# Products that nobody reads in three idle times of TensorE, in a two-layer kernel of attention and experts

## The chip, the cores and the metric

The kernel runs on one core of one Trainium2 chip. Its time is device microseconds of one launch, the median of three runs: 1240.93 us (1238.18 to 1246.87). Lower is better.

## The reference, cut to what matters

Two layers over 4 x 1024 tokens of 128 channels, each block followed by a layer norm with the residual:

```python
x = _layernorm(x + _L0_attn_ref(...))  # linear attention, elu + 1, 16 heads of 8
x = _layernorm(x + _L0_ffn_ref(...))   # 8 experts, 128 -> 512 -> 128, silu, top 2, capacity ceil(1.2 N / E)
x = _layernorm(x + _L1_attn_ref(...))  # causal softmax attention with alibi, 16 heads of 8
x = _layernorm(x + _L1_ffn_ref(...))   # 32 experts, top 4, and a shared expert
```

The third line decides most of the time: for each of 4 batches and 16 heads, 1024 x 1024 scores (the lower triangle), the largest of each query's row, exp of the difference, the product with v, and the projection. The experts of the second line each take at most a fixed number of tokens, gathered by index.

## The kernel before, in words

The program is a row of stages, each a block in which every engine has its own list of instructions; a stage ends when all engines have ended it. The stages are linear attention, routing, the first experts (`stage_experts0`), the second attention (`stage_attention`) and the second experts.

**First experts.** GpSimd (POOL) gathers 5 tiles of 128 rows for each of 8 experts, at most 2 gathers in flight. For each expert TensorE turns the 5 tiles (line 920), computes the hidden layer in four parts c = 0 to 3 of 640 columns each (512 and 128, line 935, float32), turns the tiles of the next expert, and computes the output (line 947, 20 products). ScalarE copies the turned rows (line 956) and takes silu of each part (line 968); part c = 2 waits for the silu of part 0, because two pairs of PSUM banks take turns. The order on TensorE is the order in which the code stands.

**Second attention, its start.** GpSimd gathers batch 0's expert outputs (line 1457), VectorE combines them pair by pair (line 1469, with the sums of the norm behind it), POOL takes the root (line 1443), ScalarE scales the rows (line 1406), TensorE turns them (line 1340) and makes q, k and v (lines 1343 and 1346, the list `QKV_UNITS`). ScalarE copies q and k out (lines 1395 and 1399) and splits each into three bf16 parts together with VectorE (lines 1418, 1424, 1430). SP and ScalarE issue transfers that put the parts of batch 0 into the operands `qa` and `ka` (line 1103).

**First maxima.** Attention goes in 16 steps of 4 heads. Before a step's exps, the maxima of its rows must be known: a list `MAX_UNITS` of 40 units of score products (lines 2017 for the mask and 2019), each reduced by VectorE (line 2209), and one last unit that turns the maxima (line 2006) so that they can be sent by DMA as rows of `qa` (line 1860). The units use the three PSUM banks 4, 5 and 7 in turn, so a unit's products wait until the unit three before it is reduced. For step 0 all 41 units stand ahead of the steps, and 8 units of step 1 (`EARLY`) behind them, which need the operands of step 1; these come through DRAM (`q_steps`, `k_steps`). VectorE works on other sums between these units. Inside the steps, the units of the following step stand between the score products (lines 2035 and 2039), the exps of ScalarE (line 2147) and the products with v (line 2054). Each engine has its order written out by hand; semaphores join them.

The matrix `G.ident` is a 128 x 128 identity in float32.

Of the kernel before, what the change touches and what calls it, by code (L numbers as in the profile page):

```python
# [24 lines left out]
P = 128  # L25
# [3 lines left out]
TB = SEQ // P  # L29
# [5 lines left out]
E0, H0, K0 = 8, 512, 2  # L35
# [86 lines left out]
def wait_landed(engine, landed, count):  # L122

    ahead = len(landed)
    for u in range(ahead):
        if count > u:
            engine.wait_ge(landed[u], (count + ahead - 1 - u) // ahead * 16)
# [712 lines left out]

class Weights0:


# [18 lines left out]
def stage_experts0(nc, G, I, S, W):  # L864
    HC = H0 // P
    ST = SLOTS0 // P
    FIRST = min(SLOTS0, HALF)
    PARTS = ((0, FIRST), (FIRST, SLOTS0))
    RING = 3
    with ExitStack() as ctx:  # L870
        M = Mem(nc, ctx)
        two, ring = range(2), range(RING)
        w1, w2, b1, b2, w_here = W.w1, W.w2, W.b1, W.b2, W.here
        rows = [M.sb(f"rows_{v}", [P, ST, C]) for v in ring]
        xT = [M.sb(f"exT_{u}", [P, SLOTS0]) for u in two]
        hT = M.sb("hT", [P, HC, SLOTS0])
        y = [M.sb(f"ey_{u}", [P, ST, C]) for u in two]
        landed, y_kept = [M.sem(f"landed{u}") for u in range(AHEAD)], [M.sem(f"y_kept{u}") for u in two]
        xT_psum, xT_done, h_psum, h_done = M.sem("xT_psum"), M.sem("xT_done"), M.sem("h_psum"), M.sem("h_done")
        y_psum, y_done = M.sem("y_psum"), M.sem("y_done")  # L880
        B = G.bank
        with nc.Block() as block:
            @block.gpsimd
            def _(pool):
                spaced = Spaced(pool, landed)
                for e in range(E0):
                    if e >= RING:
                        pool.wait_ge(xT_psum, e - RING + 1)
                    for s in range(ST):
                        spaced.start(out=rows[e % RING][:, s, :], out_offset=None, in_=G.x_dram,  # L890
                                     in_offset=bass.IndirectOffsetOnAxis(ap=G.token0[:, e * ST + s:e * ST + s + 1], axis=0),
                                     bounds_check=N - 1)

            @block.sync
            def _(sp):
                def keep(e):
                    sp.dma_start(G.expert_out0[e * SLOTS0:(e + 1) * SLOTS0, :].rearrange("(s p) c -> p s c", p=P),
                                 y[e % 2][:]).then_inc(y_kept[e % 2], 16)

                for e in range(2, E0):  # L900
                    sp.wait_ge(y_psum, e - 1)
                    W.load_in(sp, I, e)
                    sp.wait_ge(y_done, e - 1)
                    W.load_bias(sp, I, e)
                    keep(e - 2)
                for e in range(E0 - 2, E0):
                    sp.wait_ge(y_done, e + 1)
                    keep(e)
                for u in two:
                    sp.wait_ge(y_kept[u], E0 // 2 * 16)  # L910

            @block.tensor
            def _(pe):
                def turn(e):
                    wait_landed(pe, landed, (e + 1) * ST)
                    if e:
                        pe.wait_ge(xT_done, e)
                    for s in range(ST):
                        c, at = divmod(s * P, HALF)
                        mm = pe.transpose(B[c][:, at:at + P], rows[e % RING][:, s, :], G.ident[:])  # L920
                    mm.then_inc(xT_psum, 1)

                turn(0)
                for e in range(E0):
                    u = e % 2
                    pe.wait_ge(xT_done, e + 1)
                    pe.wait_ge(w_here[u], (e // 2 + 1) * 64)
                    for c in range(HC):
                        if c < 2:
                            if e:  # L930
                                pe.wait_ge(h_done, e * HC)
                        else:
                            pe.wait_ge(h_done, e * HC + c - 1)
                        for n, (a, b) in enumerate(PARTS):
                            mm = pe.matmul(B[2 + 2 * (c % 2) + n][:, 0:b - a], w1[u][:, c * P:(c + 1) * P],
                                           xT[u][:, a:b], start=True, stop=True)
                        mm.then_inc(h_psum, 1)
                    if e + 1 < E0:
                        turn(e + 1)
                    if e:  # L940
                        pe.wait_ge(y_done, e)
                    for s in range(ST):
                        n, at = divmod(s * C, HALF)
                        for c in range(HC):
                            if s == 0:
                                pe.wait_ge(h_done, e * HC + c + 1)
                            mm = pe.matmul(B[6 + n][:, at:at + C], hT[:, c, s * P:(s + 1) * P], w2[u][:, c, :],  # L947
                                           start=(c == 0 and at == 0), stop=(c == HC - 1), skip_group_check=True)
                    mm.then_inc(y_psum, 1)

            @block.scalar
            def _(act):
                def copy(e):
                    act.wait_ge(xT_psum, e + 1)
                    for n, (a, b) in enumerate(PARTS):
                        last = act.activation(xT[e % 2][:, a:b], B[n][:, 0:b - a], ACT.Copy)
                    last.then_inc(xT_done, 1)

                copy(0)
                for e in range(E0):  # L960
                    u = e % 2
                    act.wait_ge(w_here[u], (e // 2 + 1) * 64)
                    if e:
                        act.wait_ge(y_psum, e)
                    for c in range(HC):
                        act.wait_ge(h_psum, e * HC + c + 1)
                        for n, (a, b) in enumerate(PARTS):
                            last = act.activation(hT[:, c, a:b], B[2 + 2 * (c % 2) + n][:, 0:b - a], ACT.Silu,
                                                  bias=b1[u][:, c:c + 1])
                        last.then_inc(h_done, 1)  # L970
                    if e + 1 < E0:
                        copy(e + 1)

            @block.vector
            def _(dve):
                for e in range(E0):
                    u = e % 2
                    dve.wait_ge(y_psum, e + 1)
                    dve.wait_ge(w_here[u], (e // 2 + 1) * 64)
                    if e >= 2:  # L980
                        dve.wait_ge(y_kept[u], e // 2 * 16)
                    for n, (a, b) in enumerate(PARTS):
                        k = (b - a) // P
                        last = dve.tensor_tensor(y[u][:, a // P:b // P, :], B[6 + n][:, 0:b - a].rearrange("p (s c) -> p s c", c=C),  # L984
                                                 b2[u][:, None, :].to_broadcast([P, k, C]), ALU.add)
                    last.then_inc(y_done, 1)
# [44 lines left out]
MAX_UNITS = max_units()  # L1031
SLOTS = len(EXP_UNITS)
EARLY = 8
# [93 lines left out]
def step_plan():  # L1127

    def flags(n):
        return n == 0, n + 1 < STEPS, n + 2 < STEPS  # L1130
    count = lambda n: sum(map(len, schedule(*flags(n))))
    base = [len(MAX_UNITS) + EARLY]
    for n in range(STEPS):
        base.append(base[-1] + count(n))
    return flags, base
# [90 lines left out]
    return b == BATCH - 1 and c == 1 and kind in ("turn_att", "proj", "turn_new")  # L1226


SECOND_MOMENTS_AT = 26


# [599 lines left out]
def stage_attention(nc, G, I, S):  # L1831
# [3 lines left out]
    with ExitStack() as ctx:  # L1835
        M = Mem(nc, ctx)
        Q = Qkv(M, G.w_gu)
# [12 lines left out]
        PS, B = G.psum, G.bank  # L1850
        Q.small_read = small_read
        OUT = 6
        _, base_of = step_plan()
# [9 lines left out]
        with nc.Block() as block:  # L1863
# [121 lines left out]
            @block.tensor  # L1985
            def _(pe):
                pe.wait_ge(S.weights, 11 * 16)
                for kind, c in QKV_UNITS:
                    emit_side_tensor(pe, S, Q, (kind, 0, c))
                pe.wait_ge(G.mask_rows_here, 2 * SIDES * 16)  # L1990
# [69 lines left out]
                number = 0  # L2060
                for s, units in ((Step(0, 0, 0), MAX_UNITS), (Step(1, 1, 0), MAX_UNITS[:EARLY])):
                    for u in units:
                        emit_small(number, number % 2, s, ("max", 0, u))
                        number += 1

                def body(s, base, odd, flags):
                    pe.wait_ge(max_here[s.buf], s.used * 48 + 48)
# [89 lines left out]
            def _(dve):  # L2157
# [67 lines left out]
                for s, units in ((Step(0, 0, 0), MAX_UNITS), (Step(1, 1, 0), MAX_UNITS[:EARLY])):  # L2225
                    for u in units:
                        if number == SECOND_MOMENTS_AT:
                            dve.wait_ge(Q.summed, 4)
# [721 lines left out]
```

## Time and profile before

| | us |
|---|---|
| median of the runs | 1240.93 |
| lowest and highest run | 1238.18, 1246.87 |
| the profiled execution's own time | 1239.79 |
| its span, from first to last instruction | 1238.0 |
| TensorE busy in the span | 956.7 (77%) |
| VectorE busy | 795.7 (64%) |
| ScalarE busy | 545.5 (44%) |
| mean granted clock of TensorE | 0.878 of 2.4 GHz |

Busy time is that of instructions on an engine, matmuls with their way through the array. The granted clock is 1.00 at 2.4 GHz and 0.50 at 1.2 GHz; a value between them is a stretch with both. A line of the timeline gives the start, the time from the first start to the last end of the merged instructions, the engine, the line of the kernel, what is written from what, the shape, the count, and in brackets how long the engine had been idle and what ended that.

### The profile page before, as it was taken

What the parts mean: (1) busy time and instruction counts of PE and PEld (TensorE: products, weight loads), DVE (VectorE), ACT (ScalarE), POOL (GpSimd) and SP (SyncE); (2) the same over time, 40 slices, a digit from 0 to 9 for tenths busy, and PEclk for the clock granted to TensorE, in tenths of its full rate; (3) what the DMA queues carried; (4) which work ended last, traced back from release to release, by engine and by line L of the source; (5) the groups of instructions that cost most, each with busy time, mean ns of one, the idle gap of its engine ahead of it and who ended that gap; (6) DMA issues with size and microseconds to landing.
All of it is one profiled execution on the core that took longest, in us unless ns stands there. A gap on an engine that the chain in (4) does not pass through costs nothing. (4 is left out here: it accounts for less than half of the span.)

```text
span 1238.0 us, 20993 instructions
## 1 busy us (share of the span) xinstructions
PE 956.7 (77%) x7024; PEld 549.2 (44%) x7024; DVE 795.7 (64%) x2147; ACT 545.5 (44%) x878; POOL 488.6 (39%) x484
## 2 busy tenths in 40 slices
PE   5772118980489899998999898888889989998971
PEld 3662016760223333343334343332278868874541
DVE  4767770014397789788988888979356524554653
ACT  1331003431207667766667574555653434431241
POOL 3101045515622710262006430243545545556776
PEclk9985558995659999999989898998899999998996
DMA  4224102421311200120012222053166746541132
GB/s 119 69 69 161 30 7 79 130 71 34 88 59 35 96 29 31 43 96 28 34 41 70 79 81 80 21 156 122 53 189 190 216 138 176 170 112 43 46 83 57
DMA packets 113439, 106.19 MB, mean 86 GB/s; under 512 B 17770, under 2 KB 95210, under 8 KB 112696
## 3 DMA queue, kind: packets, MB, share of 16 engines
q1 hardware_dynamic: 74216, 65.53, 17.5%
q0 software_dynamic: 12048, 25.71, 7.7%
q10 hardware_dynamic: 27072, 13.64, 3.8%
q8 instruction: 57, 0.93, 0.3%
q14 instruction: 46, 0.38, 0.1%
HBM read 59.60 MB, written 41.94 MB: 82 GB/s over the span
## 5 line engine op out<-in xcount | busy, mean ns | idle before, releaser
L2209 DVE TENSOR_REDUCE maxima<-psum 128x1 f32<-128x512 f32 (+3 forms) x640 | 375.5, 626 | 58.8 <-PE psum L2019 57.6
L2147 ACT ACTIVATE probs<-psum 128x1024 f32<-128x1024 f32 (+3 forms) x384 | 294.5, 810 | 190.8 <-PE psum L2039 188.7
L2019 PE MATMUL psum<-ka,qa 61*128 61x512 bf16 (+3 forms) x768 | 219.7, 353 | 8.3 <-DVE maxima L2209 6.8
L2039 PE MATMUL psum<-qa,ka 64*128 64x512 bf16 (+3 forms) x768 | 169.9, 342 | 4.3 <-ACT probs L2147 3.7
L2054 PE MATMUL psum<-probs,v_wide 128*32 128x512 f32 (+3 forms) x1536 | 170.5, 518 | 0.7 <-ACT outT L2118 0.6
L1531 POOL DMA_INDIRECT sorted<-x_rows,to_row x76 | 75.9, 999 | 195.4 <-DVE to_row L1686 101.8
L2017 PE MATMUL psum<-mask 64*128 64x128 bf16 x512 | 100.1, 232 | 32.3 <-DMA qa<-max_parts 10.3
L2564 ACT ACTIVATE g_silu<-psum 128x512 f32<-128x512 f32 x80 | 47.8, 597 | 175.4 <-PE psum L2470 101.7
L1457 POOL DMA_INDIRECT w_gu<-expert_out,to_row x64 | 65.1, 1017 | 124.7 <-ACT probs L2147 84.8
L2019 PEld LDWEIGHTS psum<-ka,qa 61*128 61x128 bf16 x768 | 68.0, 98 | 96.0 <-DVE maxima L2209 73.4
L2470 PE MATMUL psum<-w_gu,g_xT 128*128 x384 | 96.8, 395 | 9.1 <-DVE g_h L2640 5.4
L2017 PEld LDWEIGHTS psum<-mask 64*128 64x128 bf16 x512 | 44.9, 97 | 132.6 <-DVE maxima L2209 88.5
L118 POOL DMA_INDIRECT f_got<-expert_out,dense x64 | 64.5, 1008 | 66.2 <-DMA f_got<-expert_out,dense 46.7
L2035 PE MATMUL psum<-mask 64*128 64x128 bf16 x512 | 85.5, 229 | 3.2 <-ACT probs L2147 2.3
L2640 DVE TENSOR_TENSOR g_h<-psum,g_silu 128x512 f32<-128x512 f32 x48 | 33.2, 691 | 77.6 <-ACT g_silu L2564 77.4
L2470 PEld LDWEIGHTS psum<-w_gu,g_xT 128*128 128x128 f32 x384 | 70.1, 192 | 25.4 <-issue 17.6
L2775 POOL DMA_INDIRECT f_got<-expert_out,dense x64 | 65.1, 1017 | 21.6 <-issue 21.6
L118 POOL DMA_INDIRECT sorted<-x_rows,to_row x52 | 51.2, 985 | 55.9 <-DMA sorted<-x_rows,to_row 38.4
L2039 PEld LDWEIGHTS psum<-qa,ka 64*128 64x128 bf16 x768 | 56.6, 98 | 29.4 <-ACT probs L2147 13.4
L984 DVE TENSOR_TENSOR ey<-psum,b 128x512 f32<-128x512 f32 (+1 forms) x16 | 7.1, 486 | 88.1 <-PE psum L947 88.1
L118 POOL DMA_INDIRECT rows<-x_dram,token x40 | 40.0, 1000 | 44.9 <-DMA rows<-x_dram,token 27.5
L2054 PEld LDWEIGHTS psum<-probs,v_wide 128*32 128x32 f32 x1536 | 31.0, 110 | 49.7 <-issue 42.1
(326 smaller groups left out, 1619.4 us busy)
## 6 DMA issues: line engine op xcount, KB each, us to landing
g_rows<-sorted SPq DMA_DIRECT2D x192, 64.0 KB
expert_out<-g_y ACTq DMA_DIRECT2D x48, 256.0 KB
w<-in_W SPq DMA_DIRECT2D x16, 256.0 KB, 3.1
w_gu<-in_gu SPq DMA_DIRECT2D x4, 1024.0 KB, 10.8
sorted<-blank SPq DMA_DIRECT2D x54, 64.0 KB
q_steps<-w_gu SPq DMA_DIRECT2D x12, 256.0 KB
k_steps<-w_gu SPq DMA_DIRECT2D x12, 256.0 KB
qa<-q_steps SPq DMA_DIRECT2D x30, 96.0 KB
```

Of the source, the lines that this page charges most:

```text
L118: self.pool.indirect_dma_start(oob_is_err=False, **transfer).then_inc(self.landed[u], 16)
L1457: pool.indirect_dma_start(out=Q.got[:, t, k, :], out_offset=None, in_=G.expert_out0, in_offset=bass.IndirectOffsetOnAxis(ap=G.to_row0[:, b ...
L1531: pool.indirect_dma_start(oob_is_err=False, **scatter_args(S, b, k, t)).then_inc(S.scattered[b // 2], 16)
L2017: pe.matmul(bank[:, (h + 1) * width - P:(h + 1) * width], G.mask[at:at + MASK_ROWS, 0, :], G.mask[at:at + MASK_ROWS, 1, :], start=(h == 0) ...
L2019: mm = pe.matmul(bank[:, h * width:(h + 1) * width], qa[b][at:at + ROWS_MAX, (h0 + h) % PER_SIDE, qt * P:(qt + 1) * P], ka[b][at:at + ROWS ...
L2035: pe.matmul(B[score_bank(h)][:, 0:P], G.mask[at:at + MASK_ROWS, 1, :], G.mask[at:at + MASK_ROWS, 0, :], start=True, stop=False, skip_group ...
L2039: mm = pe.matmul(B[score_bank(h)][:, 0:(c + 1) * HALF - q0], ka[s.buf][at:at + ROWS_ALL, h % PER_SIDE, j * P:(j + 1) * P], qa[s.buf][at:at ...
L2054: mm = pe.matmul(B[OUT][32 * h:32 * (h + 1), q0 - c * HALF:HALF], v_wide[s.buf][:, j, h, PAD * (1 - c):PAD * (1 - c) + 32], probs[k % PRIN ...
L2147: act.activation(probs[k % PRING][:, 2 * pair:2 * pair + 2, 0:w], PS[:, 2 * pair:2 * pair + 2, 0:w], ACT.Exp).then_inc(exps, 1)
L2209: dve.tensor_reduce(maxima[:, seg, h0:h0 + heads, qt], bank[:, 0:heads * width].rearrange("p (h k) -> p h k", h=heads), AX.X, ALU.max).the ...
L2470: mm = pe.matmul(B[1 + s // 2][:, at:at + 2 * H1], xT[n % 2][:, s * P:(s + 1) * P], w_gu[:, bass.ds(experts[n][s] * (2 * H1), 2 * H1)], st ...
L2775: pool.indirect_dma_start(oob_is_err=False, **transfer).then_inc(here, 16)
```

## The change

A helper issues `count` products of the identity with itself into the first 128 columns of a bank, and nobody reads them. It is called in three places of TensorE's list: 22 products at the start of the first experts, ahead of the first turn; 16 products at the start of the second attention, behind a new wait for the last pair of batch 0's gathers (the wait that VectorE has too); and one product behind each of the last 20 of the 49 units of the first maxima (units 29 to 48, counted from 0). The banks are 7, 4 and 3; bank 3 is not in the units' turn, and bank 4 is not used by the first q and k units.

```diff
+def emit_filling(pe, G, bank, count):
+
+    for _ in range(count):
+        pe.matmul(bank[:, 0:P], G.ident[:], G.ident[:], start=True, stop=True)
...
+                emit_filling(pe, G, B[7], 22)
                 turn(0)
                 for e in range(E0):
...
+FILLED_UNITS = 20
...
                 pe.wait_ge(S.weights, 11 * 16)
+                pe.wait_ge(Q.got_here[TB // 2 - 1], 2 * K0 * 16)
+                emit_filling(pe, G, B[4], 16)
                 for kind, c in QKV_UNITS:
                     emit_side_tensor(pe, S, Q, (kind, 0, c))
...
                     for u in units:
                         emit_small(number, number % 2, s, ("max", 0, u))
                         number += 1
+                        if number > len(MAX_UNITS) + EARLY - FILLED_UNITS:
+                            emit_filling(pe, G, B[3], 1)
```

## Rows read from the trace of the kernel before

**Rows 1.** The page, part 2: TensorE's granted clock in 40 slices of the span.

```profile
PEclk9985558995659999999989898998899999998996
```

**Rows 2.** Windows: start and end, length, busy time of each engine, clock, DMA.

```profile
189.66:196.10 6.44, 5.58 (x13) 3.12 (x13) 0.00 (x0) 2.42 (x4) 3.98 (x4) 0.50 0.15 41
307.30:314.60 7.30, 6.88 (x16) 3.42 (x16) 0.00 (x0) 4.60 (x9) 4.09 (x4) 0.66 0.12 28
343.00:360.00 17.00, 15.46 (x47) 3.88 (x46) 16.96 (x45) 0.00 (x0) 5.85 (x4) 0.50 0.19 65
360.30:363.70 3.40, 0.37 (x1) 0.10 (x1) 2.41 (x8) 0.00 (x0) 0.44 (x2) 0.50 0.09 37
363.80:367.50 3.70, 3.63 (x24) 1.56 (x25) 3.10 (x7) 0.00 (x0) 0.00 (x0) 0.50 0.09 10
```

**Rows 3.** Windows about two falls of the clock, at 276 and at 430 us.

```profile
276.00:278.00 2.00, 0.00 (x0) 0.00 (x0) 0.54 (x2) 0.00 (x0) 0.19 (x1) 1.00 0.09 27
...
430.00:430.50 0.50, 0.29 (x2) 0.01 (x1) 0.50 (x2) 0.00 (x0) 0.50 (x1) 1.00 0.13 49
431.50:432.00 0.50, 0.00 (x0) 0.00 (x0) 0.00 (x0) 0.00 (x0) 0.50 (x1) 0.78 0.13 49
```

**Rows 4.** Timeline, from the end of routing into the first experts.

```profile
178.67 0.18 DVE L839 CAST token<-owner 128x40 uint32<-128x40 f32 x1
...
180.21 1.16 POOL L118 DMA_INDIRECT rows<-x_dram,token  x1 [10.19 <-issue]
...
189.66 1.33 PE L920 MATMUL psum<-ident,rows 128*128 128x128 f32 x5 [11.79 <-DMA rows<-x_dram,token]
...
191.85 4.59 PE L935 MATMUL psum<-exT,w 128*128 128x512 f32 x8 [0.85 <-ACT exT L956]
...
195.09 0.99 POOL L118 DMA_INDIRECT rows<-x_dram,token  x1 [0.32 <-issue]
...
195.73 1.78 ACT L968 ACTIVATE hT<-psum,b 128x512 f32<-128x512 f32 x4
...
196.72 2.43 PE L935 MATMUL psum<-exT,w 128*128 128x512 f32 x8 [0.29 <-ACT hT L968]
...
198.99 0.71 PE L920 MATMUL psum<-ident,rows 128*128 128x128 f32 x5
...
199.54 4.72 PE L947 MATMUL psum<-w,hT 128*128 128x128 f32 x40
```

**Rows 5.** The gathered rows by tile: time from issue to landing.

```profile
DMA to landing us min/median/max: 2.5/2.6/2.7
```

**Rows 6.** Groups by form, TensorE, from 189 to 197 us.

```profile
L920 PE MATMUL psum<-ident,rows 128*128 128x128 f32 x5 | 1.3, 432 | 11.8 <-DMA rows<-x_dram,token 11.8
```

**Rows 7.** Timeline, start of the second attention.

```profile
300.58 0.61 DVE L1469 SCALAR_TENSOR_TENSOR w_gu<-w_gu,gate,x_rows 128x128 f32<-128x128 f32 x2 [3.45 <-DMA w_gu<-expert_out,to_row]
...
305.57 3.19 ACT L1406 ACTIVATE x_rows<-w_gu,shift_q,rstd_q 128x128 f32<-128x128 f32 x8 [36.52 <-POOL shift_q L1445]
...
307.36 1.09 PE L1340 MATMUL psum<-ident,x_rows 128*128 128x128 f32 x4 [34.20 <-ACT x_rows L1406]
...
309.72 1.92 PE L1343 MATMUL psum<-side_xT,wq_sb 128*128 128x512 f32 x2
...
314.64 0.69 ACT L1399 ACTIVATE w_gu<-psum,bk_sb 128x512 f32<-128x512 f32 x1 [0.17 <-PE psum L1343]
```

**Rows 8.** Timeline, TensorE in the first maxima and into the first step.

```profile
351.90 0.28 PE L2017 MATMUL psum<-mask 64*128 64x128 bf16 x1
...
359.56 0.29 PE L2017 MATMUL psum<-mask 64*128 64x128 bf16 x1
...
363.78 0.30 PE L2017 MATMUL psum<-mask 64*128 64x128 bf16 x2 [1.53 <-DMA ka<-k_steps]
...
368.10 0.63 PE L2039 MATMUL psum<-qa,ka 64*128 64x512 bf16 x1
...
368.53 0.34 PE L2035 MATMUL psum<-mask 64*128 64x128 bf16 x2
```

## The prediction

> **What bounds the kernel now.** I read the page's clock line first. It says where TensorE runs at half speed: from slice 4 to slice 6, from 9 to 11, and then only here and there [rows 1]. The added products can pay in one way alone, by having the clock at 2.4 GHz when real work comes, so the question for each place is what TensorE's speed decides just behind it. The windows answer that for four stretches at 0.50: the first expert's start, the first q and k (0.66, so partly), the first maxima, and the eight units of step 1 [rows 2]. In the maxima, from 343 to 360 us, VectorE is busy 16.96 of 17.00 us, so it is the bound there; in the eight units, from 363.80, TensorE is busy 3.63 of 3.70 us and is itself the bound. The timelines then give what waits for what. The two windows about falls of the clock matter last: there I read how long an idle time the high clock survives.
>
> **The cost of one product.** The output product of the experts is the nearest in form: the code has 20 of them for an expert and the trace 40 instructions in 4.72 us at the high clock, so each product is two instructions of 0.118 us, 0.24 us in all [rows 4]. For the low clock the nearest row is the turn, five single instructions in 1.33 us with a mean of 0.432 each; (1.33 - 0.43) / 4 = 0.22 us from start to start [rows 4, 6]. So a product at the low clock takes 0.44 us. The bounds are the ratio of the clocks on 0.236 (0.47) and the turn's whole mean of 1.33 / 5 = 0.27 an instruction (0.53).
> The Trainium skill, page "TensorE: Matmul & The Clock Gate", section "Back-to-back issue gap", gives 107 ns for 128 columns at the low clock; its text there does not speak of float32. By it a product would cost a quarter of what I take, the loss in the third place below would fall from 0.8 us to about nothing, and the sum would be -1.7 us. The rows on float32 decide for me, and the page's figure enters nothing else.
>
> **Place 1, the first experts.** 22 products start when TensorE enters the stage, between VectorE's last instruction (178.67 + 0.18 us) and POOL's first gather (180.21). All at the low clock they take 9.7 us and end at 188.5 to 189.9; the rows that the turn waits for are there at 189.66 [rows 4]. So their own cost is hidden by the gathers, but for 0.2 us at the worst. The gain, if the clock is high and stays high: the turn takes 0.71 for 1.33 us, the copy behind it 0.86 as before, part 0 ends about 1.1 us sooner, and part 2 follows it by the same 2.5 us (table load and silu). Part 2 then starts near 194.9 instead of 196.72, and the turn of the second expert could start at 197.2 instead of 198.99. It can't: its last gather starts at 195.09 and lands 2.6 us later, at 197.69 [rows 4, 5]. **The gain is at most 198.99 - 197.69 = 1.3 us**; the gathers are late next.
> Does the clock stay high? In the trace the first expert ran from 191.85 us on and the clock was low until 196.10, 4.3 us in [rows 2, 4]. If it rises about as late into the added products, the 12 that are left go at 0.24 us, and all end at 186 to 187.4 us, 2.3 to 3.6 us ahead of the rows; if later, closer to them. In the trace such an idle time went both ways: after the products that ended at 273.16 us (34.20 us ahead of the turn at 307.36) the clock was still 1.00 from 276 to 278 [rows 3, 7], and after the stop near 430.3 us it was falling by 432.0 [rows 3]. So the high clock survives between under 2 and over 4 us of idle time. The place of the stop decides, and that is chance from run to run. I take half: **-0.65 us**, ends -1.3 and +0.2.
>
> **Place 2, the second attention.** The new wait is for the same gathers as VectorE's, which passes at 300.58 us. Behind it on TensorE stand only the q, k and v units, and the first of these waits for ScalarE until 307.36 [rows 7]. 16 products at the low clock take 7.0 us and end at 307.6: hidden, but for 0.25 us. The gain: from 307.30 to 314.60 the clock is 0.66 on the mean, so 32% of the 7.3 us went at the high level and 5.0 us at the low one, with TensorE busy 6.88 us [rows 2]. The second turn needs the last scaled rows, at 305.57 + 3.19 = 308.76 us, whatever the clock; so 1.4 us of the 5.0 can't shrink, and half of the other 3.6 is 1.8 us. By it the last copy of k starts near 312.9 instead of 314.64 [rows 7]. Behind this copy are the splits and the transfers into `qa` and `ka`, one after the other on ScalarE and SP, and everything follows them. POOL's gathers of batch 1 don't move, since they wait for the scaled rows; they now meet the transfers elsewhere, which may take some of the gain. The idle time between the products' end and the turn is shorter than in place 1, 0 to 1.5 us, but the turns are short too and have gaps between them, so the clock can still fall. I take **-1.1 us**, ends -1.8 and +0.25.
>
> **Place 3, the first maxima.** Here the products stand between real ones. Units 29 to 39 start 7.66 us apart for 10, 0.77 us each, by VectorE's pace [rows 8]. At the low clock such a unit costs TensorE 0.43 us for 512 columns (368.10 to 368.53) and about 0.1 more where it has the mask [rows 8]; with 0.44 for the product that is 0.87 to 0.97 us, more than VectorE takes. Over ten units that is 1 to 2 us, less what TensorE is ahead (two units lie ready in the other banks): 0 to 1 us, and nothing once the clock is high, since 0.5 us is then under 0.77. Then the maxima are turned and step 1's operands waited for; from 360.30 to 363.70 TensorE is busy 0.37 us, and the product behind unit 39 and the one behind the turned maxima add 0.5 to that [rows 2]. An idle time of some 2.5 us in pieces: the clock falls in most runs, by the two examples. Then come eight units whose products fill TensorE wholly at the low clock, 3.7 us, and the change adds 8 x 0.44 = 3.5 us to them. At the high clock the same is 1.9 + 8 x 0.24 = 3.8 us, as long as before: no gain in the units, but up to 0.8 us in the scores behind them, for whose start ScalarE waits. Between these ends, with the clock rising somewhere in the eight units because they are dense now, half the added time remains, less the faster scores: **+0.8 us**, ends -0.8 and +4.5.
>
> The 116 added instructions and their weight loads are under 1% of TensorE's; the trace has no row that prices fetching them, and I take nothing, with the noise of the runs over it. Nothing else moves: banks 7, 4 and 3 are not waited for, no other engine's list changes, and no DMA is added.
>
> **The sum.** -0.65 - 1.1 + 0.8 = -0.95 us. Against the profiled execution's 1239.79 us (1238.0 of span and 1.8 around it) that is 1238.8; this execution is 1.1 us under the median, so for the median of the runs **1240.0 us**. All stages behind are in a chain with these, so what is won or lost here reaches the end.
>
> **The rivals.**
> 1. *The clock stays high from each set of products through the work behind it.* For it: the sets end close to the work, and at 276 us the clock outlived 3 us of idle time [rows 3]. Against: the idle time left in place 1, and that in front of the eight units. It gives -1.3 - 1.8 - 0.8 = -3.9, so 1237.0 us. Chance 0.3.
> 2. *The eight units of step 1 run at the low clock with a product behind each, and the products, not the maxima, set the start of step 0's scores.* Place: 363.8 to 367.5 us. Price +3.5, and up to 1.0 more in units 29 to 39, with nothing won in places 1 and 2: 1244.4 to 1245.4 us. It decides when the clock is at 0.50 for more than some 5 us from 363.8 on. For it: from 343 to 360 TensorE was busy 91% by the same count and the clock stayed at 0.50 all the way [rows 2]. Against: float32 products with the whole array leave no gap. Chance 0.2.
> 3. *The products don't bring the clock up in time anywhere* (it rises where it rose before) and the maxima hide theirs: 1240.9 us, no change. Chance 0.1.
> My forecast, the clock partly kept, has 0.4.
>
> **How the numbers follow.** The lowest case (1237.0) with the runs' own reach below their median (2.8 us) gives 1234; the highest (1245.4) with a part of the reach above it gives 1247. So 1234 to 1247 us. A measurement of this kernel can tell about 1%, 12 us, from no change. No case comes near that on either side; what is left is the unknown, such as a late stretch whose clock happens to turn out otherwise: faster by over 1% 0.04, within 1% 0.93, slower by over 1% 0.03.
>
> **What would show it.** Place 1: the clock at 189.66 us, the start of the second expert's turn (198.99 before; not under 197.7), and its wait then put down to the gathers. Place 2: the last copy of k at 313 instead of 314.6, counted from VectorE's first combine, and the first maxima's unit as much sooner. Place 3: the spacing of units 29 to 39 (0.77), the clock at the first unit of step 1, and the time from that unit to the first scores (3.7 to 4.3 us before). I am wrong if the clock is not at 1.00 when the real work begins in places 1 and 2, if the products end behind it, or if a stretch outside the three moves by more than they do together.

## The result, and the profile after

| | before | with the products |
|---|---|---|
| median of 20 runs, us | 1241.41 (1236.07 to 1248.34) | 1247.11 (1239.66 to 1255.54) |
| ratio, 95% interval | | 1.0052 (1.0035 to 1.0070) |
| the profiled execution's span, us | 1238.0 | 1245.8 |
| TensorE busy, us | 956.7 | 980.6 |
| mean granted clock | 0.878 | 0.882 |

The change makes the kernel 0.5% slower, 6.5 us by the ratio (5.7 by the two medians); forecast were 1 us less and 1234 to 1247 us. In the clock line of the page the first twelve digits are what they were: the low stretches of the first experts, of the second attention's start and of the first maxima are all still there [rows 1]. Slice 13, which holds the first steps, has fallen from 9 to 8.

```profile
PEclk9985558995658989999999898898799989999995
```

**Place 1.** The timeline after, of the first experts, answers to [rows 4]. The 44 instructions take 6.71 us, as forecast (part at each clock). The rows come 3.75 us behind their end; by then the clock is low again, and the turn takes 1.33 us, as before. The second expert's turn is 18.98 us behind POOL's first gather (180.47); before it was 18.78.

```profile
179.67 6.71 PE L846 MATMUL psum<-ident 128*128 128x128 f32 x44 [1.54 <-PEq L698]
...
190.12 1.33 PE L926 MATMUL psum<-ident,rows 128*128 128x128 f32 x5 [3.75 <-DMA rows<-x_dram,token]
...
199.45 0.71 PE L926 MATMUL psum<-ident,rows 128*128 128x128 f32 x5
```

**Place 2.** The second attention after, which answers to [rows 7]. The products end at 307.47, ahead of the turn, which takes 0.66 us for 1.09. The last copy of k starts 12.46 us behind VectorE's first combine of the last pair, for 14.06 before: 1.6 us won.

```profile
301.65 0.61 DVE L1477 SCALAR_TENSOR_TENSOR w_gu<-w_gu,gate,x_rows 128x128 f32<-128x128 f32 x2 [3.45 <-DMA w_gu<-expert_out,to_row]
...
301.69 5.78 PE L846 MATMUL psum<-ident 128*128 128x128 f32 x32 [27.47 <-DMA w_gu<-expert_out,to_row]
...
308.35 0.66 PE L1348 MATMUL psum<-ident,x_rows 128*128 128x128 f32 x4 [0.89 <-ACT x_rows L1414]
...
314.11 0.69 ACT L1407 ACTIVATE w_gu<-psum,bk_sb 128x512 f32<-128x512 f32 x1 [0.17 <-PE psum L1351]
```

**Place 3.** Two units in the maxima after, with weight loads (PEld). A 512-column product starts at 355.01, the added one's weight load only at 355.54, and the next unit at 356.27. So the added product holds TensorE 0.73 us, and the product before it 0.53 where it held it 0.43 [rows 8]. VectorE's reduce now waits for TensorE (the last row; in brackets 0.42 us).

```profile
355.00 0.10 PEld L2029 LDWEIGHTS psum<-ka,qa 61*128 61x128 bf16 x1 [0.23 <-issue]
355.01 0.60 PE L2029 MATMUL psum<-ka,qa 61*128 61x512 bf16 x1
...
355.54 0.50 PEld L846 LDWEIGHTS psum<-ident 128*128 128x128 f32 x2 [0.44 <-issue]
355.54 0.79 PE L846 MATMUL psum<-ident 128*128 128x128 f32 x2
...
356.27 0.60 PE L2029 MATMUL psum<-ka,qa 61*128 61x512 bf16 x1
...
356.80 0.79 PE L846 MATMUL psum<-ident 128*128 128x128 f32 x2
356.91 0.69 DVE L2221 TENSOR_REDUCE maxima<-psum 128x1 f32<-128x512 f32 x1 [0.42 <-PE psum L2029]
```

The end of the maxima and the first scores after. Unit 39 starts at 364.15, 28.5 us behind the first unit's product (335.65); before it was 23.25 (336.31 to 359.56) [rows 8]. Units 41 and 42 start 1.26 us apart. TensorE does not wait for step 1's operands any more (1.53 us before [rows 8]).

```profile
364.15 0.28 PE L2027 MATMUL psum<-mask 64*128 64x128 bf16 x1
...
366.91 0.28 PE L2027 MATMUL psum<-mask 64*128 64x128 bf16 x1
...
368.17 0.28 PE L2027 MATMUL psum<-mask 64*128 64x128 bf16 x1
```

And ScalarE's first exps after, in the same view:

```profile
378.70 2.73 ACT L2159 ACTIVATE probs<-psum 128x1024 f32<-128x1024 f32 x3 [49.14 <-PE psum L2049]
```

The first exp is at 378.70, 43.0 us behind the first unit's score product; before it was 32.4 (from 336.37 to 368.77). The windows after, with columns as in [rows 2], show the clock (the third number from the end). It is 1.00 from 183.6, and low again from 190, when the rows come. It is 1.00 with q and k. And it is 0.50 in the two windows of the maxima, though TensorE is busy 10.50 of 10.50 us (the last window) with units 41 to 48 and the products among them.

```profile
183.60:185.60 2.00, 2.00 (x20) 2.00 (x20) 0.00 (x0) 0.00 (x0) 1.17 (x2) 1.00 0.11 33
190.00:192.00 2.00, 1.33 (x5) 0.93 (x5) 0.00 (x0) 0.52 (x2) 1.00 (x1) 0.50 0.13 33
307.50:315.00 7.50, 4.98 (x17) 2.43 (x18) 0.00 (x0) 6.37 (x14) 3.47 (x4) 1.00 0.10 22
351.70:366.50 14.80, 14.21 (x41) 7.00 (x41) 10.12 (x31) 0.00 (x0) 2.28 (x3) 0.50 0.15 51
366.90:377.40 10.50, 10.50 (x41) 5.94 (x40) 5.15 (x11) 0.00 (x0) 0.00 (x0) 0.50 0.15 48
```

### The profile page after: what moved, and what is told of

The parts are those of the page before. It is cut to its first block and busy times, and to the rows that moved or that the text cites. A ratio compares the mean times of both kernels' runs of the same rounds, so it can differ in the third digit from the quotient of the medians.

```text
span 1245.8 us, 21225 instructions
## 1 busy us (share of the span) xinstructions
PE 980.6 (79%) x7140; PEld 569.3 (46%) x7140; DVE 797.1 (64%) x2147; ACT 545.9 (44%) x878; POOL 491.5 (39%) x484
## 5 line engine op out<-in xcount | busy, mean ns | idle before, releaser
L2482 PEld LDWEIGHTS psum<-w_gu,g_xT 128*128 128x128 f32 x384 | 70.5, 193 | 25.3 <-issue 17.4
## 6 DMA issues: line engine op xcount, KB each, us to landing
w_gu<-in_gu SPq DMA_DIRECT2D x4, 1024.0 KB, 10.9
```

The source lines that it names most:

```text
L2482: mm = pe.matmul(B[1 + s // 2][:, at:at + 2 * H1], xT[n % 2][:, s * P:(s + 1) * P], w_gu[:, bass.ds(experts[n][s] * (2 * H1), 2 * H1)], st ...
```

## The experiments

Four marks are read from each trace: the second expert's turn, from POOL's first gather; the last copy of k, from the first combine of the last pair; and the 40th reduce and the first exp, each from the first unit's score product. The marks are those of one profiled execution of each kernel, the ratios those of 7 to 20 runs of it, against the kernel before on the same chip, with 95% intervals.

| kernel | second turn | copy of k | 40th reduce | first exp | ratio |
|---|---|---|---|---|---|
| before | 18.8 | 14.1 | 24.2 | 32.4 | |
| all three places | 19.0 | 12.5 | 29.2 | 43.0 | 1.0052 (1.0035 to 1.0070) |
| place 1 | 18.8 | 14.6 | 24.2 | 32.7 | 0.9997 (0.9972 to 1.0023) |
| place 2 | 18.8 | 12.5 | 24.2 | 33.0 | 0.9977 (0.9954 to 1.0000) |
| place 3 | 19.0 | 14.3 | 29.2 | 43.0 | 1.0068 (1.0044 to 1.0093) |
| places 1 and 2 | 17.4 | 12.5 | 24.2 | 36.4 | 0.9973 (0.9941 to 1.0006) |
| place 3 in bf16 | 18.9 | 14.4 | 27.4 | 39.8 | 1.0046 (1.0023 to 1.0068) |
| behind units 41 to 48 | 18.7 | 14.3 | 24.3 | 39.4 | 1.0062 (1.0031 to 1.0093) |
| place 1 with 34 | 17.7 | 14.9 | 24.2 | 32.8 | 0.9985 (0.9961 to 1.0009) |
| a block ahead of the maxima | 18.8 | 14.5 | 24.1 | 32.5 | 0.9976 (0.9949 to 1.0004) |
| 34 in place 1, and place 2 | 19.6 | 12.5 | 24.2 | 34.0 | 0.9986 (0.9958 to 1.0013) |
| a block of 8 behind unit 48 | 18.9 | 14.3 | 24.2 | 35.6 | 0.9999 (0.9967 to 1.0031) |
| all blocks | 17.6 | 12.5 | 24.0 | 34.8 | 0.9992 (0.9963 to 1.0022) |
| two behind each of 41 to 48 | 18.7 | 14.0 | 24.2 | 42.9 | 1.0062 (1.0031 to 1.0093) |

### One place at a time

The theory (A) was that place 3 makes the whole loss, because a product alone between bf16 products costs some 0.8 us; the rival (B), that the loss is spread. Each kernel keeps one of the calls, or two:

```diff
 # place 1 alone
-                pe.wait_ge(Q.got_here[TB // 2 - 1], 2 * K0 * 16)
-                emit_filling(pe, G, B[4], 16)
...
-                        if number > len(MAX_UNITS) + EARLY - FILLED_UNITS:
-                            emit_filling(pe, G, B[3], 1)
```

> Only the 22 products ahead of the first experts. Theory A (a product between the bf16 units costs some 0.8 us of TensorE's time, and place 3 alone makes the loss): no loss here, and no gain where the clock falls in the 3.7 us between the products' end and the rows, as in the changed kernel's profile; 0 to -1.3 us, turn of the second expert at 10 us behind POOL's first gather start or up to 1.3 earlier. Rival B (the loss is spread: added instructions and another pattern of the clock in the stages behind): +1 to +3 us here.

> Only the 16 products at the start of the second attention, with their wait. Theory A: the last copy of k starts 1.6 us sooner after VectorE's first combine of the last pair, and the kernel is 1 to 2 us faster (ratio 0.998 to 1.000). Rival B: no gain or +1 to +3 us, since the later clock pattern gives back what is won.

> Only the 20 single products in the first maxima. Theory A: the whole loss and more, the first exp 9 to 11 us later against the first maxima's unit than before, the time +6 to +10 us (ratio 1.005 to 1.008), the clock at 0.50 over units 29 to 48. Rival B: +1 to +3 us, as for each of the others.

> The 22 and the 16 products, without those in the maxima. Theory A: 1 to 3 us faster than before (ratio 0.9975 to 0.9995). Rival B: +2 to +5 us.

Place 3 alone has the whole loss, 1.0068, and both of its marks to a tenth of a microsecond as with all three. Places 1 and 2 have none of it. Place 2's 1.6 us are there each time; the kernels without it have the copy of k at 14.0 to 14.9, so the gain is 1.6 us or a little more. B is out.

In the fourth kernel the clock stayed high in place 1 (second turn at 17.4), with the same 22 products as the first. What differs is the idle time behind them: the clock rose later among them, so that they took 8.08 us (7.08 in the first kernel, 6.71 in the changed one), and the rows came 2.03 us behind their end, for 3.31 and 3.75 where the clock fell. Up to this point the first and the fourth kernel have the same instructions, so this is chance from run to run.

```profile
186.37 0.77 PE L926 MATMUL psum<-ident,rows 128*128 128x128 f32 x5 [2.03 <-DMA rows<-x_dram,token]
```

But the fourth kernel's first exp is late, at 36.4, without a product in the maxima. The row of it says why: the first unit of step 1 waited 5.54 us for the operands of step 1, where it was 1.53 before [rows 8].

```profile
359.54 0.30 PE L2027 MATMUL psum<-mask 64*128 64x128 bf16 x2 [5.54 <-DMA ka<-k_steps]
```

The first maxima started sooner (32.4 us behind the combine, for 35.8), and the transfers through DRAM did not keep up. Counted from the combine, the first exp comes 68.8 us behind, for 68.2 before: by then all that place 2 had won is lost in this execution. What place 1 won lies ahead of the combine and is not touched by it.

### What makes a product dear

Place 3 alone, with four bf16 products in place of each float32 one:

```diff
+def emit_filling_bf16(pe, G, bank, count):
+    for _ in range(count):
+        pe.matmul(bank[:, 0:P], G.before_b[:], G.before_b[:], start=True, stop=True)
...
-                            emit_filling(pe, G, B[3], 1)
+                            emit_filling_bf16(pe, G, B[3], 4)
```

> Only place 3, and each float32 product there replaced by four bf16 products of 128 columns (a 128 x 128 matrix of zeros and ones), which stream as many columns as the two passes of two take. Theory A1 (the price of 0.83 us is that of float32 weight loads and passes that overlap with nothing beside bf16 products): a unit of 512 columns then comes every 0.95 to 1.0 us at the low clock, not every 1.26, and the first exp is 3 to 5 us later than before against the first unit, not 10. Theory A2 (the price is that of four passes of 128 columns, however they are loaded): every 1.2 us or more, and +9 to +10.

The result lies between the two theories: a unit of 512 columns comes every 1.08 us, and the first exp 7.4 us late.

The timeline of TensorE in that kernel, with one weight load:

```profile
360.26 0.60 PE L2032 MATMUL psum<-ka,qa 61*128 61x512 bf16 x1
360.79 0.35 PEld L852 LDWEIGHTS psum<-before_b 128*128 128x128 bf16 x4 [0.44 <-issue]
360.80 0.61 PE L852 MATMUL psum<-before_b 128*128 128x128 bf16 x4
361.34 0.60 PE L2032 MATMUL psum<-ka,qa 61*128 61x512 bf16 x1
361.88 0.61 PE L852 MATMUL psum<-before_b 128*128 128x128 bf16 x4
```

The four take 0.54 us (360.80 to 361.34), and the product before them again 0.54; a unit's product with as many columns, 512, takes 0.43 where such units follow each other [rows 8]. So some 0.1 us is lost on each side of a change between the units' products and the added ones, in bf16 too; float32 adds 0.2 more (0.73 for 0.54), and why it does is open.

Then, again without places 1 and 2, the product behind the last 8 units only, two of it there, and eight in one block:

```diff
-FILLED_UNITS = 20
+FILLED_UNITS = 8
...
 # two behind each:
-                            emit_filling(pe, G, B[3], 1)
+                            emit_filling(pe, G, B[3], 2)
...
 # in one block:
-                        if number > len(MAX_UNITS) + EARLY - FILLED_UNITS:
-                            emit_filling(pe, G, B[3], 1)
+                        if number == len(MAX_UNITS) + EARLY:
+                            emit_filling(pe, G, B[3], FILLED_UNITS)
```

> Only place 3, and a product behind the last 8 units alone (41 to 48), not behind 29 to 40. By the prices seen in the changed kernel's trace these 8 make 5 us of the 10 by which the first exp is late: the 40 reduces keep 24.2 us, the first exp +4.5 to +5.5, ratio 1.002 to 1.004. If instead what went before (the clock held low, VectorE late) makes units 41 to 48 slow: under +2 us.

> Only place 3: two float32 products behind each of the units 41 to 48. Theory A: the second one has its like before it and costs 0.43 us, so the first exp comes 8 x 0.43 = 3.4 us later than with one behind each: 42.5 to 43 us behind the first unit's product. Rival (each costs 0.85): 46 us. If the denser stream brings the clock up within these units: under 42 us.

> Only place 3: eight float32 products in one block behind unit 48, not one behind each of the units 41 to 48. Theory A (a product costs 0.43 us at the low clock in a row of its like, and another 0.4 where bf16 products stand before and behind it): the first exp 36 to 36.5 us behind the first unit's product, where it is 32.4 without products and 39.4 with one behind each unit. Rival: a product costs 0.85 us in this place however it stands; 39 us.

One behind each costs 7.0 us at the first exp, 0.87 a product, more than I expected: in the changed kernel the units 29 to 39 were so late that the wait for the operands was gone, and here it is still there (1.72 us) and nothing absorbs. With the products TensorE is the bound in these units, so a product costs all the time that it takes.

Two behind each: 42.9, as expected; the second costs 3.5 / 8 = 0.44 us. The pair takes 1.15 us (376.54 to 377.69), for 0.73 with one, so the second takes 0.42. The ratio is 1.0062 with one and with two: these 7 and 8 runs, with an interval of 3.8 us to either side, do not show the 3.5 us that the traces do.

TensorE with two behind each:

```profile
376.54 1.22 PE L846 MATMUL psum<-ident 128*128 128x128 f32 x4
377.69 0.28 PE L2024 MATMUL psum<-mask 64*128 64x128 bf16 x1
```

Eight in one block: 35.6, a little under what was expected, with the time as before (0.9999). The block holds TensorE for 3.59 us, from 367.34 to the next unit's mask at 370.93 (not shown), which is 0.45 a product. At the first exp only 3.2 us of it are left, since the scores behind the block ran at the high clock (0.38 us, where they took 0.63 [rows 8]). That is not to the block's credit: the clock rose between 370 and 371 us in both executions, and with the block the scores stand behind that time.

TensorE with the block, and the scores behind it:

```profile
367.34 3.66 PE L846 MATMUL psum<-ident 128*128 128x128 f32 x16
...
371.01 0.38 PE L2046 MATMUL psum<-qa,ka 64*128 64x512 bf16 x1
...
371.28 0.37 PE L2046 MATMUL psum<-qa,ka 64*128 64x512 bf16 x1
```

**So a product costs 0.42 to 0.45 us among its like, and 0.83 to 0.87 alone between bf16 products, at the low clock.** A figure of 0.85 for every product is out.

### Whether the high clock can be kept

```diff
-                emit_filling(pe, G, B[7], 22)
+                emit_filling(pe, G, B[7], 34)
```

> Only place 1, with 34 products instead of 22, so that they end nearer to the rows. If the idle time of 3.7 us between products and rows is why the clock fell: the clock is 1.00 at the first turn, and the second expert's turn starts 17.4 us behind POOL's first gather, where it is 18.8 without (the gathers allow no less); 1 to 1.5 us faster at the end of the stage. If the clock never rises in some runs, all 34 take 14.6 us and the turn is 4.5 us late. Rival: the clock falls in the turn's own gaps; then 18.8 stays.

The products end 0.59 us ahead of the turn, the clock is 1.00 from 191 to 200 us, the turn takes 0.76 us, and the second expert's turn comes at 17.7: 1.1 us won, with the gathers as the next bound. The ratio, 0.9985, has 1 in its interval.

The timeline of that kernel's TensorE:

```profile
184.76 9.77 PE L846 MATMUL psum<-ident 128*128 128x128 f32 x68 [1.54 <-PEq L698]
...
195.12 0.76 PE L926 MATMUL psum<-ident,rows 128*128 128x128 f32 x5 [0.59 <-DMA rows<-x_dram,token]
```

```diff
                 for kind, c in QKV_UNITS:
                     emit_side_tensor(pe, S, Q, (kind, 0, c))
+                emit_filling(pe, G, B[3], 22)
                 pe.wait_ge(G.mask_rows_here, 2 * SIDES * 16)
```

> None of the three places; 22 products in one block behind the v units, ahead of the first maxima, where TensorE has 7.5 us to wait for the operands. Theory A: hidden by the wait; the block brings the clock up, the maxima are VectorE's pace anyway (24.2 us for 40 reduces as before), and if the clock falls again among them nothing is won: 0 to -1 us. Rival: with the clock high the maxima are faster than VectorE's pace seemed to allow, 22 us or less.

The first products of the maxima ran at the high clock (0.24 us for 0.30), and by 342.54 the next took 0.28 again. The 40 reduces took 24.1 us: VectorE's pace, whatever the clock. The ratio of 0.9976 would be 3 us, more than the 0 to 1 us that I expected, and up to the first exp (32.5 for 32.4) the trace shows no gain; where it comes from is open, and its interval reaches 1.0004.

Then the parts that won, together. The first of these two kernels is the one that the second text calls the first:

> Places 1 and 2 without 3, with 34 products in place 1. Theory A: the two gains add: second expert's turn 17.4 to 17.7 us behind POOL's first gather, last copy of k at +12.5 us behind the fourth combine; 2 to 4 us faster than before, ratio 0.997 to 0.998. Rival B: what is won ahead of the maxima is lost in the wait for step 1's operands, whose transfers don't come sooner: ratio 0.999 to 1.000.

> 34 products in place 1, 16 in place 2, and 22 in one block behind the v units, none in the maxima. As the first of this call, with nothing more won: the block is hidden by the wait for the operands, and the clock falls again within the maxima, so 24.0 to 24.3 us for 40 reduces; ratio within 0.001 of the first of this call. Rival: the block's end comes behind the operands now that these are 1.6 us sooner, and costs up to 1 us.

Neither is clear of the kernel before (0.9986 and 0.9992). In the first one's trace the rows themselves came late (turn at 10.9 us behind the first gather, for 9.5), 2.37 us behind the end of the products. The turn still ran at the high clock (0.77 us); the clock fell in the hidden layer behind it, and the second turn came at 19.6, later than before. Place 2 won its 1.6 us, and the first exp was at 34.0 for 32.4. In the second, both gains were there (17.6 and 12.5), and the first exp came at 34.8.

The wait for the operands of step 1 was 3.17 and 4.20 us in these two, for 1.53 before [rows 8]. It takes back what the sooner start of the maxima had won beyond place 2's 1.6 us, and sometimes more. Counted from the combine, the first exp comes at 66.7 us with place 2 alone and in the first of these two, at 67.6 in the second and at 68.8 with places 1 and 2; it was at 68.2 before. So place 2's gain reached the first exp almost whole in two executions, in part in one, and not at all in one. The experiments point to no version that is surely faster than the kernel before: place 2 alone comes nearest, and its interval touches 1.0000.

## Why the prediction was wrong

- **The cost of one product: the step that failed.** I took 0.44 us from rows of products that stand among their like, and used it in all three places. It holds at the low clock among their like (0.42 to 0.45), and in places 1 and 2, partly at the high clock, the products stayed within it (22 in 6.71 us, 16 in 5.78). In place 3 it was 0.83: 0.73 us from its weight load to the next unit, and 0.10 more on the product before it. My upper bound of 0.53 was from the same kind of row and did not bound this. No row before showed a float32 product between bf16 ones in this place, and I should have said so: the sequence was not priced, only the instruction. The 107 ns of the Trainium skill, page "TensorE: Matmul & The Clock Gate", section "Back-to-back issue gap", which would have made place 3 free, were still farther off than my 0.44 us.
- **What makes the sequence dear, as far as the traces show it.** Weight loads that wait. The Trainium skill, page "TensorE: Matmul & The Clock Gate", section "The mechanism", says that a weight load overlaps with running products only where it is for another group of rows. The trace does not agree: from 183.60 to 185.60 us of the changed kernel, among products that all take the same 128 rows, TensorE and its weight loads are both busy 2.00 of 2.00 us, so the loads ran under products for the same rows. What the traces show is that a load waits where an operand on all 128 rows follows one on a half of them. The kernel puts two heads of a step on rows 0 to 63 and two on rows 64 to 127, and a unit's operands take 61 or 64 rows of one half. The identity's load, on 128 rows, starts only when the unit's 512-column product is 0.53 us old, and so does the load of 128 bf16 rows (360.79, behind a product started at 360.26). Within a unit of the kernel before, the load of the mask's 64 rows stands at the start of a product on 61 rows of the same half:

```profile
364.96 0.42 PE L2019 MATMUL psum<-ka,qa 61*128 61x256 bf16 x1
364.97 0.15 PEld L2017 LDWEIGHTS psum<-mask 64*128 64x128 bf16 x1
```

  That the rows of the array decide is argued from these lines and not tested: no run has the added products on one half of the rows.
- **Place 3, units 29 to 39.** Forecast 0 to 1 us; 5.0 measured (29.2 for 24.2). With 1.26 to 1.37 us a unit against VectorE's 0.77, the two units in hand are soon used up.
- **Place 3, units 41 to 48.** I had TensorE as the bound there, since it was busy 3.63 of 3.70 us, and half of 3.5 us as the cost. That reading of the bound does not hold for the kernel before. The units take the two halves of the rows in turn, and the first two of them ran side by side (both have their mask products in the row of 363.78 in [rows 8]). It is VectorE's reduces that stand there without a gap, ten of them:

```profile
364.40 5.12 DVE L2209 TENSOR_REDUCE maxima<-psum 128x2 f32<-128x256 f32 x10 [0.96 <-PE psum L2019]
```

  With a product on all 128 rows behind each, no two units run side by side and TensorE is the bound. The cost was 7.0 alone, and 5.6 in the changed kernel (43.0 - 29.2 - 8.2), since the wait for the operands was used up before.
- **Place 3, the clock.** I let it rise within these units. It did not, up to 380 us, two us behind them. From 351.7 to 366.5 TensorE was busy 14.21 of 14.80 us at 0.50. That is a second step that failed: that the units would bring the clock up because they are dense now, and, against rival 2, that float32 products with the whole array leave no gap. Of the 9.8 us between my +0.8 and the measured 10.6, 3.7 lie below my upper end of 4.5, which stood for the low clock all the way; the 6.1 above it are the price of the product.
- **Place 1.** Forecast half of 1.3 us, with chance deciding. With 22 products nothing was won in the changed kernel and alone, and 1.4 us in the kernel with places 1 and 2. With 34 it was 1.1 and 1.2 us in two kernels, and a loss of 0.8 in the third, where the rows came late. The mechanism and its bound by the gathers were right.
- **Place 2.** Forecast 1.1 us, measured 1.6 in every kernel that has it, near the end of 1.8. That the wait for the operands of step 1 can take it back before the first exp I did not name.
- **The sum.** With the measured prices: 0 - 1.6 + 10.6 = +9.0 us; by the first exp the changed kernel is 8.9 us behind, counted from the combine (77.1 for 68.2). At the end of this one pair of executions it is 7.8 from the start of the span, or 6.7 counted from the combine, which was itself 1.1 us late; by the ratio it is 6.5 (4.3 to 8.7). Between them lie stretches of low clock later in attention, which differ from execution to execution; whether they give the 2 us back on the mean is not shown.
- **The rivals.** Rival 2 was right in its place and its mechanism (chance 0.2), and short in its price for the same reason; it had nothing won in place 2, where 1.6 us were. The other rivals are out. Slower by 0.5% is within 1%, as forecast, with the time 0.1 us above the range. That the time comes so near the range is no support for the sum, which had the wrong sign: the range reached so far by rival 2.

## What to carry to other kernels

Price an added instruction in the sequence in which it will stand: here a float32 product among its like cost half of what it cost between bf16 ones. Work that fills an idle time should stand in one block inside that time and end just before the real work, and not between the products of an engine that is or becomes the bound. Do not take a high busy share as the sign of the bound; look whose instructions follow each other without a gap. And ask what the raised clock is to speed up: where VectorE set the pace, or a transfer was late next, little or nothing was won here.

## What the runs showed of the hardware

A row of 44 float32 instructions, started at 0.50, had the clock at 1.00 by 183.6 us, 4 us later. Behind such a row in place 1, the turn of five tiles ran at the high clock after 0.53, 0.59, 2.03 and 2.37 us of idle time (0.76 to 0.77 us), in part after 3.31 (0.92 us), and at the low one after 3.75 (1.33 us).

With the mix of float32 and bf16 products the clock stayed at 0.50 from 351.7 to 377.4 us, with TensorE shown as busy for 96% to 100% of it. Busy time in the profile was no sign here that the clock would rise.

Weight loads ran under the products before them where both took all 128 rows, and where both took the same half of them. Where 128 rows followed a 512-column product on 61, in float32 and in bf16 alike, the load came 0.53 us behind that product's start. Two units on different halves of the rows ran side by side: their mask products started within 0.02 us of each other (363.78 and 363.80).
